# A graph network with two message-passing layers: another placing of the node units, another order within a step, and a small-row store cut in 28

## The reference

```
h  = relu(layernorm(x))
x1 = x + relu(relu((h + sum over edges of relu(h[src]) into dst) @ W1 + b1) @ W2 + b2)
h1 = relu(layernorm(x1))
x2 = x1 + hop_layer(h1)      # queries, keys, values; three hops of messages over the edges
```

## Time and profile before

| | |
|---|---|
| median of 3 runs | 1816.73 us |
| lowest, highest | 1809.44, 1824.96 us |
| the profiled execution's own time | 1815.59 us |
| its span | 1812.7 us |
| DVE busy over the span | 1488.8 us (82%) |
| PE busy over the span | 1345.3 us (74%) |
| ACT busy over the span | 1015.2 us (56%) |
| granted TensorE clock, mean | 0.860 |

### The profile page before, as it was taken

How to read it: one execution, slowest core, us unless ns; L and a number is a source line. 1 busy time by engine, 2 the same in 40 slices (tenths; PEclk the granted TensorE clock), 3 DMA queues, 4 the chain that set the end, 5 groups by cost and what they waited for, 6 DMA issues and landing times. The chain is left out here.

```text
span 1812.7 us, 22165 instructions
## 1 busy us (share of the span) xinstructions
PE 1345.3 (74%) x5794; PEld 840.3 (46%) x5794; DVE 1488.8 (82%) x3207; ACT 1015.2 (56%) x2815; POOL 1193.0 (66%) x1185
## 2 busy tenths in 40 slices
PE   3666778788888985777777277778577898877772
PEld 3455666665666664454544033333233344455551
DVE  5866777789989886799999799999456788699992
ACT  4556878768878875455554255555355556333330
POOL 7775666616665531777773577777477777777776
PEclk9787898879978877798998589888799999988886
DMA  4394333334655554699998588888435554466650
GB/s 126 77 51 123 102 104 102 91 94 132 149 134 141 133 135 92 213 323 319 320 318 293 177 288 305 307 309 299 152 98 159 146 160 135 128 174 175 173 152 17
DMA packets 280787, 313.83 MB, mean 173 GB/s; under 512 B 168577, under 2 KB 198137, under 8 KB 268118
## 3 DMA queue, kind: packets, MB, share of 16 engines
q1 hardware_dynamic: 223734, 246.39, 45.3%
q0 software_dynamic: 56928, 66.04, 14.6%
HBM read 214.54 MB, written 161.32 MB: 207 GB/s over the span
## 5 line engine op out<-in xcount | busy, mean ns | idle before, releaser
L924 PE MATMUL bank<-product,ident 128*128 128x512 f32 (+1 forms) x800 | 383.3, 637 | 134.9 <-DVE product L1278 134.9
L533 POOL DMA_INDIRECT state<-state_hop,slot_of_src x392 | 395.6, 1009 | 126.1 <-issue 108.5
L703 ACT ACTIVATE bank<-state,norm 128x512 f32<-128x512 f32 x392 | 251.1, 679 | 254.9 <-DMA state<-state_hop,slot_of_src 221.6
L1278 DVE TENSOR_TENSOR product<-bank,queries 128x512 f32<-128x512 f32 x392 | 261.2, 687 | 90.0 <-ACT bank L703 88.3
L924 PEld LDWEIGHTS bank<-product,ident 128*128 128x128 f32 x800 | 160.9, 206 | 356.0 <-issue 182.7
L495 POOL DMA_INDIRECT x_edges<-in_x,dst_tiles x196 | 199.5, 1018 | 156.9 <-DVE x_edges L1188 97.0
L509 POOL DMA_INDIRECT row_of_src<-node_rows,pos_int x196 | 195.2, 996 | 122.2 <-DMA node_rows<-row_new 62.8
L495 POOL DMA_INDIRECT x_edges<-in_x,src_tiles x196 | 203.1, 1036 | 95.8 <-issue 54.4
L549 POOL DMA_INDIRECT out<-rows,dst_out x196 | 193.1, 985 | 59.7 <-issue 50.0
L831 PE MATMUL bank<-dst_steps,from_here 128*128 128x197 f32 x392 | 98.6, 406 | 101.7 <-ACT row_no L645 75.2
L1276 DVE SCALAR_TENSOR_TENSOR acc<-acc,same_as_before,bank 128x512 f32<-128x512 f32 x196 | 145.2, 741 | 15.9 <-ACT bank L703 15.1
(11 more groups left out here) (220 smaller groups left out, 3033.0 us busy)
## 6 DMA issues: line engine op xcount, KB each, us to landing
state_hop<-acc SPq DMA_DIRECT2D x98, 1024.0 KB, 4.7
x_nodes<-in_x SPq DMA_DIRECT2D x49, 256.0 KB, 3.6
src_row<-in_src_row SPq DMA_DIRECT2D x49, 256.0 KB, 3.6
out<-out_rows SPq DMA_DIRECT2D x49, 256.0 KB
dst_row<-in_dst_row SPq DMA_DIRECT2D x49, 256.0 KB, 4.5
kv_rows<-kv SPq DMA_DIRECT2D x49, 256.0 KB, 3.5
gg<-head_sums SPq DMA_DIRECT2D x98, 128.0 KB
kv_back<-kv_rows SPq DMA_DIRECT2D x49, 256.0 KB
```

The source lines that it names most:

```text
L533: pool.indirect_dma_start(out=mg[u % 4][:, k, :], out_offset=None, in_=d_m[hop - 1], in_offset=bass.IndirectOffsetOnAxis(ap=sidx[:, t:t + ...
L703: act.activation(pw[t % len(pw)][:, :], mg[u % 4][:, k, :], ACT.Copy, scale=wn12[:, t:t + 1]).then_inc(weighted, 1)
L924: ins = ten.matmul(ph[:, 0:k * D].rearrange("p (c j) -> p c j", j=HD), ident[:, :], part, start=(r == 0), stop=(r == HD - 1))
L1278: vec.tensor_tensor(ihj(pr[m % 2][:, u % 2 * EH + k, :]), ihj(pw[t % len(pw)][:, :]), over_j(Q[:, t, :]), ALU.mult).then_inc(multiplied, 1)
```

## The change

Node units get other ticks: two in three ticks up to tick 48 (32 units), then 51, 53, 55, 57, and from 61 to 97 every third tick. Statistics get columns of their own for x1 of a node unit, since both sums can now fall into one tick. On ACT the root L650 and the search's signs (one tick later than before) move ahead of the normalisation. On DVE x1 of a node unit moves ahead of the sums, and the four selections of 128 columns become one operation on 512, behind the variance. On PE the search's matmuls move behind the node units' W1 and W2; the second turn of the early units goes to bank 7, and each turn waits only for the copies of its own bank. The ring of x gets 5 buffers, and a load is issued 3 ticks ahead in place of 4. The store of the two numbers becomes 28 stores of 7 columns, in ticks 12 to 39.

```diff
 RT = 5
-RX = 4
+RX = 5
+R1 = 4
 NR = 12
-COLS = HT + 2 * EH
+E1, E2 = 2 * HT, 2 * HT + EH
+COLS = 2 * HT + 2 * EH
 
 B0 = AU
 S0 = B0 + 4
@@ -59,16 +61,22 @@
     if (g >= E0 + CU + 2 or (g - E0) % 3 == 1) and len(F_STEP) < CU + 7:
         F_STEP[g] = len(F_STEP) - 3
 END = max(F_STEP)
-DENSE_TICKS = [2 * k for k in range(1, DU + 1)]
-assert len(DENSE_TICKS) == DU and all(t % 2 == 0 for t in DENSE_TICKS)
+DENSE_TICKS = [t for t in range(2, B0 + 1) if t % 3 != 1]
+for t in range(B0 + 2, C0):
+    if t - DENSE_TICKS[-1] >= (2 if t < B0 + 10 else 3) and (t - 5 <= B0 or t - 5 not in DENSE_TICKS):
+        DENSE_TICKS.append(t)
+DENSE_TICKS = DENSE_TICKS[0:DU]
+assert len(DENSE_TICKS) == DU
+TAIL = 7
+TAIL_AT = {12 + i: i * TAIL for i in range(T // TAIL)}
 DENSE_AT = {t: m for m, t in enumerate(DENSE_TICKS)}
 
 
 def stats_at(g):
 
     dense, edge, edge2 = g in DENSE_AT or g - 5 in DENSE_AT, 0 <= g - 1 < 2 * AU, AU <= g - 9 < 2 * AU
-    lo = 0 if dense else HT if edge else HT + EH
-    hi = HT + 2 * EH if edge2 else HT + EH if edge else HT
+    lo = 0 if dense else E1 if edge else E2
+    hi = COLS if edge2 else E2 if edge else E1
     return (lo, hi) if dense or edge or edge2 else None
 
...
         ptd, pad_, pbd, pvd = bank[0:4]
+
+        def turn2_bank(m):
+
+            return bank[7] if DENSE_TICKS[m] <= B0 else ptd
+
+        LATE = len([t for t in DENSE_TICKS if t <= B0])
...
                     load_srow(g + 2)
-                m = DENSE_AT.get(g + 4)
+                m = DENSE_AT.get(g + 3)
                 if m is not None and m > 1:
                     load_x(m)
                 u = g + 2 - S0
                 if 0 <= u < AU:
                     load_drow(u)
-                if g == 12:
+                if g in TAIL_AT:
+                    c = slice(TAIL_AT[g], TAIL_AT[g] + TAIL)
                     sync.wait_ge(tail_set, 2)
-                    sync.dma_start(by_slot(d_tab)[:, :, D:TW], tail[:, :, :]).then_inc(tail_kept, 16)
+                    sync.dma_start(by_slot(d_tab)[:, c, D:TW], tail[:, c, :]).then_inc(tail_kept, 16)
                 if g == B0 + 3:
                     sync.wait_ge(normed_e, AU)
                     for c in range(2):
...
             pool.wait_ge(pos_set, 1)
-            pool.wait_ge(tail_kept, 16)
+            pool.wait_ge(tail_kept, 16 * len(TAIL_AT))
             for b in range(3):
                 pool.wait_ge(t_kept[b], landed(AU - 1, b, 3))
...
+                    act.activation(hT2d[:, :], turn2_bank(m)[:, :], ACT.Relu).then_inc(copied2_d, 1)
                 m = DENSE_AT.get(g - 3)
                 if m is not None:
                     act.wait_ge(mm1_d, m + 1)
...
 
+                if g in STAT_NO:
+                    lo, hi = stats_at(g)
+                    act.wait_ge(varred, STAT_NO[g] + 1)
+                    act.activation(q[:, 3, lo:hi], q[:, 2, lo:hi], ACT.Sqrt, bias=epsc[:, 0:1],
+                                   scale=1.0 / (D * D)).then_inc(rooted, 1)
+                u = g - 3
+                if 0 <= u < CU:
+                    act.wait_ge(searched, u + 1)
+                    for k in range(EH):
+                        t = u * EH + k
+                        each = pair[:, 256 * k:256 * k + T]
+                        act.activation(each, each, ACT.Sign, bias=spm[:, t:t + 1],
+                                       scale=-1.0, accum_out=signs[:, t:t + 1])
+                    act.activation(rowno[:, u * EH:(u + 1) * EH],
+                                   pair[:, :].rearrange("p (k c) -> p k c", c=256)[:, :, T], ACT.Copy).then_inc(counted, 1)
                 if g - 1 in STAT_NO:
                     act.wait_ge(scaled, STAT_NO[g - 1] + 1)
                 u = g - 10 - B0
                 if 0 <= u < AU:
...
-                u = g - 2
-                if 0 <= u < CU:
-                    act.wait_ge(searched, u + 1)
...
-                if g in STAT_NO:
-                    lo, hi = stats_at(g)
-                    act.wait_ge(varred, STAT_NO[g] + 1)
...
                     ins.then_inc(fixes, 1)
-                u = g - 2
-                if 0 <= u < CU:
-                    ten.wait_ge(g_set, u + 1)
-                    wait(ten, counted, u)
-                    for k in range(EH):
-                        ins = ten.matmul(pair[:, 256 * k:256 * k + T + 1], gsel[u % 2][:, k * P:(k + 1) * P], delta[:, :],
-                                         start=True, stop=True, skip_group_check=True)
...
                     rows_out(pbd, a1d, W2, 0, HT // 2, mm2_d)
+                u = g - 2
+                if 0 <= u < CU:
+                    ten.wait_ge(g_set, u + 1)
+                    wait(ten, counted, u)
+                    for k in range(EH):
+                        ins = ten.matmul(pair[:, 256 * k:256 * k + T + 1], gsel[u % 2][:, k * P:(k + 1) * P], delta[:, :],
+                                         start=True, stop=True, skip_group_check=True)
+                    ins.then_inc(searched, 1)
                 m = DENSE_AT.get(g - 6)
                 if m is not None:
                     ten.wait_ge(h1_d, m + 1)
-                    turn_dense(2, h1d[m % 2], turned2_d)
+                    if m == 0:
+                        ten.wait_ge(prep_v, 3)
+                    if m >= LATE:
+                        wait(ten, copied1_d, len([t for t in DENSE_TICKS if t + 1 < g]))
+                    wait(ten, copied2_d, m)
+                    turn_dense(turn2_bank(m), h1d[m % 2], turned2_d)
                 m = DENSE_AT.get(g - 1)
                 if m is not None:
                     ten.wait_ge(normed_d, m + 1)
-                    turn_dense(1, zd[m % 2], turned1_d)
+                    wait(ten, copied1_d, m)
+                    late = len([t for t in DENSE_TICKS if t + 6 < g])
+                    if late > LATE:
+                        wait(ten, copied2_d, late)
+                    turn_dense(ptd, zd[m % 2], turned1_d)
 
                 if g == 6:
                     ten.matmul(pprep[:, 0:P], dpm[:, 0:1].to_broadcast([P, P]), ident[:, :], start=True, stop=True)
...
-                    select(1)
...
+                m = DENSE_AT.get(g - 4)
+                if m is not None:
+                    vec.wait_ge(mm2_d, m + 1)
+                    wait(vec, res_d, m - R1 + 1)
+                    vec.scalar_tensor_tensor(flat(x1d[m % R1][:, 0, :, :]), pbd[:, :], 0.0, flat(xn[m % RX][:, 0, :, :]),
+                                             ALU.max, ALU.add).then_inc(x1_d, 1)
                 if g in STAT_NO:
                     lo, hi = stats_at(g)
                     m, m2, e, u = DENSE_AT.get(g), DENSE_AT.get(g - 5), g - 1, g - 9 - B0
...
-                    select(1)
+                u = g - S0
+                if 0 <= u < AU:
+                    vec.wait_ge(drow_in[u % 3], landed(u, u % 3, 3))
+                    wait(vec, turned_e, u - 1)
+                    vec.tensor_tensor(sel[u % 2][:, :].rearrange("p (k c) -> p k c", c=P),
+                                      drow[u % 3][:, :].rearrange("p (k c) -> p k c", c=P),
+                                      tmf[:, u * EH:(u + 1) * EH].unsqueeze(2).to_broadcast([P, EH, P]),
+                                      ALU.is_equal).then_inc(s_set, 1)
...
```

More of the change, by code:

```diff
@@ L630, in _ @@
                     act.wait_ge(x1_d, m + 1)
-                    act.activation(x1d[m % RX][:, 1, :, :], x1d[m % RX][:, 0, :, :], ACT.Square).then_inc(squared2_d, 1)
+                    act.activation(x1d[m % R1][:, 1, :, :], x1d[m % R1][:, 0, :, :], ACT.Square).then_inc(squared2_d, 1)
                 if g == B0 + 3:
@@ L750, in _, with turn_dense @@
         def _(ten):
-            turned = {1: 0, 2: 0}
             def bias(which, n):
                 return b3[:, which * P:(which + 1) * P].unsqueeze(1).to_broadcast([3, n, P])
-            def turn_dense(which, what, done):
-                wait(ten, copied1_d, turned[1])
-                wait(ten, copied2_d, turned[2])
+            def turn_dense(p, what, done):
                 for k in range(HT // 2):
-                    ins = ten.transpose(ptd[:, k * P:(k + 1) * P], what[:, 2 * k:2 * k + 2, :], ident[:, :])
+                    ins = ten.transpose(p[:, k * P:(k + 1) * P], what[:, 2 * k:2 * k + 2, :], ident[:, :])
                 ins.then_inc(done, 1)
-                turned[which] += 1
             def rows_out(p, lhs, w, which, n, done):
@@ L781, in _ @@
                     wait(ten, x1_e, u)
+                    if u == 0:
+                        ten.wait_ge(copied2_d, LATE)
                     rows_out(pbe, a1e, W2, 0, EH // 2, mm2_e)
@@ L1099, in _ @@
                 qp, q = st[(g - 1) % RS], st[g % RS]
[L1100 to L1109, removed]
-                        for k in range(n_sel, n_sel + n):
-                            t = u * EH + k
-                            ins = vec.tensor_scalar(sel[u % 2][:, k * P:(k + 1) * P], drow[u % 3][:, k * P:(k + 1) * P],
-                                                    tmf[:, t:t + 1], None, ALU.is_equal)
```

(22 more changed lines are left out.)

27 lines of the change are left out of this document (7 added, 20 removed).

## The result

The changed kernel takes 1842.62 us (median of 4 runs, 1837.15 to 1846.58), the kernel before 1818.92 (4 runs). The ratio is 1.013, 95% interval 1.008 to 1.019: slower by 1.3%. The forecast was 1820 us and "no change" (50%), with 24% for slower by over 1%. The range (1788 to 1848) held the time; the forecast's own narrower range (1804 to 1835) did not.

What follows compares the result with a forecast made beforehand. DVE was taken to set the pace, in a loop of waits with ACT. 1815.6 - 18.0 + 22.3 + 10 + 0 - 19.4 + 8 = 1818.5 us profiled, about 1820 as median; range 1788 to 1848, the forecast's own 1804 to 1835.

Steps and rivals of the forecast that it cites:

- Term 1: Store in 28 parts: the stall of the single store goes and the parts cost nothing, -18.0 us.
- Term 2: First gathers, ticks 12 to 50: the way between variances leads through ACT's root, signs, normalisation, squares; +22.3 us.
- Term 6: Both gather stretches: PE's search matmuls run partly at the lower clock, 4 us in each, +8 us.
- rival 2: PE's clock decides: search matmuls at the lower clock delay ACT's copies and the root; 1845 us, chance 18%.
- Term 3: Start, ticks 1 to 12: eight units begin instead of six, and the degrees' root waits longer; +10 us.
- Term 4: Ticks 50 to 61: units two ticks apart as before, 0 us, bounds -4 to +4.
- Term 5: Second gathers, ticks 61 to 99: a node unit every third tick, mean 6.18 us a tick, -19.4 us.
- Rival 1: First gathers and start: the new order frees DVE, whose waits go with nothing in their place; 1789 us, chance 24%.
- Rival 3: The 28 store parts are not hidden: the stall's 18 us return as held loads; 1838 us, chance 8%.

Runs made afterwards that it cites:

- e1: The kernel before with only the single store split into 28 stores; ratio to the kernel before 0.991.
- e5: The changed kernel with PE's preparatory matmuls of tick 6 ahead of the search matmuls; ratio to the kernel before 1.003.
- e2: The changed kernel with one store again in place of 28; ratio to the kernel before 1.022.
- e10: The kernel before with the 28 stores and ACT's root moved ahead of the square of x1 and the signs; ratio to the kernel before 0.962.
- e7: The changed kernel with ACT's root late (just ahead of the square of x1) and DVE's result rows early; ratio to the kernel before 0.956.
- e6: The changed kernel with DVE's result rows right behind the reciprocal and shift, not behind the variance; ratio to the kernel before 1.009.
- e3: The changed kernel with the node units in the old ticks 2, 4, ..., 98; ratio to the kernel before 1.021.
- e4: The changed kernel with ACT's root behind signs, normalisation and edge copies, just ahead of the square of x1; ratio to the kernel before 0.984.

## Why the prediction was right or wrong

- **The sum.** By the profiled executions the forecast was +3 and the outcome +21.6 us. The likeliest case was "no change" within 1%; the measured 1.3% is just above that, and its interval (0.8 to 1.9%) begins below it. The missing 19 us are Terms 3, 4 and 5 and the end, as follows. That the wide range held the time is partly luck: its upper part, and the 24% for slower by over 1%, had been given to rivals 2 and 3, and neither of them made this kernel slow.
- **Term 1, the store: right.** -18.0 forecast, -17.4 in e1.
- **Term 2, the first gathers: right.** 268.5 forecast (260.2 - 18.0 + 22.3 + 4), 267.3 measured; each of the three ticks is within 0.1 us. Of the 4 us for the clock (half of Term 6) some 3 came, as three ticks of 8.1 and 8.4 us. In the one from 312.98 us PE had run the search matmuls (2.47 us in place of 1.60) and the turns (1.06 in place of 0.60) at the lower level, ACT waited 2.17 us for the turns, and its root started 1.1 us after the variance. That is rival 2's mechanism, but in a few ticks and not in a third of them. ACT's copies waiting for the turns, the sign named for that rival, did appear (28.0 us in 23 waits); in the regular periods ACT still had to wait for the variance behind them, or started the root some 0.3 us after it (0.2 without such a wait), so they cost little.
- **Term 3, the start: mis-sized, the largest miss.** +10 forecast with a bound of 13, +17.9 measured. I had costed the move of the search matmuls in general, and not what is queued behind them in tick 6. DVE makes its preparation out of two matmuls that stand behind the search; the search now waits for ACT's signs, and those for DVE's variance. Before the change DVE didn't wait for those matmuls. The wait for ACT's root of the degrees was 3.75 where it had been 0.46, so it added 3.3 and not the 2 of the sum.

```profile
59.55 0.16 DVE L1009 COPY next_first<-bank 128x1 f32<-128x1 f32 x1 [6.29 <-PE bank L892]
...
75.46 1.38 DVE L1040 RECIPROCAL dinv_slots<-prep_tmp 128x196 f32<-128x196 f32 x1 [3.75 <-ACT prep_tmp L670]
```

  e5 takes 7.3 us of this back (4.5 beside e2). DVE's added work, forecast at 8.0 us, was 9.1 by its busy time. The rest was not split further.
- **Term 4, ticks 50 to 61: mis-sized.** 0 forecast, bound 4, +5.9 measured, and e2 and e5, with the same code here, took the same (78.0 and 77.9 us). Two ticks hold most of it: 11.9 us for 9.6 at the exchange of the edge sums at the tile ends, and 9.9 for 7.3. In both, DVE waited (8.0 and 3.4 us) for a W2 product that PE made at the lower level. In the first, PE had stood 7.2 us for the exchanged sums, where it had stood 3.7 before the change. Why the exchange came later was not looked into, and no run changes this place alone:

```profile
411.43 0.76 PE L812 MATMUL bank<-ident,h_edges 128*128 128x128 f32 x2 [7.22 <-DMA h_of_src<-tile_fixes]
...
419.10 0.69 DVE L1147 SCALAR_TENSOR_TENSOR x_nodes<-bank,x_nodes 128x512 f32<-128x512 f32 x1 [7.98 <-PE bank L781]
```

- **Term 5, the second gathers: right in its ticks, short in the clock.** 6.6, 6.7 and 5.2 or 5.3 us in the fast periods, for 6.62, 6.62 and 5.29. In five of the thirteen periods the third is 6.9, PE being at the lower level (granted clock 0.85): 242.7 in place of 238.8 (254.2 - 19.4 + 4).
- **Behind tick 99**, taken at 0: +3.3 us, of which 1.7 behind tick 106; not looked into, and within what two readings of the same code differ by (1128.2 us in the kernel before and 1139.1 in e1).
- **Rival 1 (the new order frees DVE)** did not happen, for the reason given; e10, and e7 beside e6, show that it is what another place of the root gives.
- **Rival 2 (PE's clock)** did not decide the changed kernel, but it is in Terms 4 and 5 and the odd ticks of Term 2, and e3 and e4 show it at full size; e3 was itself mispriced by leaving it out.
- **Rival 3 (the parts are not hidden)** is refuted by e1.

So, beside e1, which has the store's 17.4 us: the first gathers lose 24.5 us by order and placing (267.3 for 242.8); beside the kernel before the start loses 17.9, ticks 50 to 61 lose 5.9, what follows tick 99 3.3, and the second gathers gain 11.5. 24.5 - 17.4 + 17.9 + 5.9 + 3.3 - 11.5 = 22.7, the difference of the spans. Whether the search matmuls' new place costs anything beside the start was not tried by itself.

## What to carry to other kernels

Take an operation that another engine stands still for, here ACT's root. It belongs behind what its own engine can do before its input is there (the normalisation), and ahead of what waits for that other engine's later results (the square of x1) or is merely long (the signs). That place was worth 2 to 3% (e10 against e1) with one block of code moved. The changed kernel put it ahead of the normalisation too. e4 put it behind the normalisation again, but in an order where another wait, for a shared bank, then came out. For a moved step, follow the queue in the odd ticks too (preparation, exchanges), not only in the steady period. And after opening one loop, read the waits again: what it had covered (here a bank shared by neighbouring units) can then cost as much, and be worth as much.

## What the runs showed of the hardware that I had not expected

The same eight matmuls of a Wv product take 1.16 or 2.08 us, by the level of the clock. Waits of 2.4 and 4.0 us on PE stood ahead of a lower stretch in e3 and e4, but in the changed kernel waits of 2.84 and 2.85 us were followed by the full clock once and by the lower one once, so the runs don't show what length of wait it takes. The placing of work on other engines moved the granted clock of the second gathers between 0.75 (e6) and 0.99 (e4) with the same matmuls, and with it 261.2 against 200.3 us. And behind one store of 25,088 pieces of 8 bytes SP's next DMA stood at its issue for 28.9 us before the change and 38.6 us in e2, while DVE waited 17.9 and 32.5 us for a result store; 28 stores of the same bytes landed in 3.9 to 4.6 us each (e1) and took nothing from any tick.
